# Four graph layers on one core: chunked normalising with ScalarE products at the end of the message layer, and a rearranged prologue of the polynomial layer

## What is computed

```
def _L2_gnn_ref(mu, x, edge_index, edge_w, W1, W2, W3, W4):
    ...
    agg = jax.ops.segment_sum(cat_feat, src, num_segments=n_nodes)
    agg = relu(agg @ W4.T)
    return relu(h_x + h_mu + agg)

def _L3_gnn_ref(x, W, bias, edge_index, num_nodes):
    ...
    deg = jax.ops.segment_sum(ones, row, num_segments=num_nodes)
    dinv = jnp.where(deg > 0, 1.0 / jnp.sqrt(jnp.where(deg > 0, deg, 1.0)), 0.0)
    norm = dinv[row] * dinv[col]

    def L_apply(h):
        msg = norm[:, None] * h[col]
        return h - jax.ops.segment_sum(msg, row, num_segments=num_nodes)
    ...
    for k in range(K + 1):
        out = out + h_k @ W[k] * inv_f
        if k < K:
            h_k = -T * L_apply(h_k)
            inv_f = inv_f / (k + 1)
    return out + bias
...
x = _layernorm(x + _L2_gnn_ref(x, node_vec1, edge_index, edge_weight, ...), axis=-1)
x = _layernorm(x + _L3_gnn_ref(x, L3_gnn_W, L3_gnn_bias, edge_index, 3125), axis=-1)
```

## Time and profile before

| what | value |
|---|---|
| median of three runs | 1601.18 us |
| profiled execution, own time | 1603.67 us |
| its span, first to last instruction | 1601.5 us |
| mean granted TensorE clock | 0.961 of full |
| TensorE busy | 1395.6 us (87%) |
| VectorE busy | 1232.4 us (77%) |
| ScalarE busy | 594.9 us (37%) |
| GpSimd busy | 44.4 us (3%) |

### The profile page before, as it was taken

The page is one execution under the profiler, slowest core; times in us unless marked ns, Lnnn a source line. Parts: engine busy times, 40 slices in busy tenths (PEclk is TensorE's granted clock), DMA queues, the critical chain, the costliest instruction groups (busy, mean ns, idle before and its releaser), DMA issues. The chain is left out here.

```text
span 1601.5 us, 44020 instructions
## 1 busy us (share of the span) xinstructions
PE 1395.6 (87%) x16795; PEld 1291.0 (81%) x16795; DVE 1232.4 (77%) x3606; ACT 594.9 (37%) x1073; POOL 44.4 (3%) x82
## 2 busy tenths in 40 slices
PE   0745468879987999999999979699999999999997
PEld 0434456669986888888888849599999999999997
DVE  4999988865446888888888867667777687677676
ACT  0249779971105777777777740100000000000000
POOL 2111100000000000000000000000000000000000
PEclk9989989989998999999999979689999999999999
DMA  1000035541005445454232260000000000000000
GB/s 20 9 1 0 0 91 157 158 129 33 2 15 152 127 133 153 114 152 114 83 106 75 63 152 2 6 2 2 2 2 2 2 2 2 2 2 2 2 6 19
DMA packets 37008, 83.91 MB, mean 52 GB/s; under 512 B 22941, under 2 KB 23957, under 8 KB 36863
## 3 DMA queue, kind: packets, MB, share of 16 engines
q1 hardware_dynamic: 33617, 81.46, 18.2%
q10 hardware_dynamic: 3024, 0.39, 0.2%
q0 software_dynamic: 224, 0.13, 0.1%
HBM read 60.76 MB, written 21.14 MB: 51 GB/s over the span
## 5 line engine op out<-in xcount | busy, mean ns | idle before, releaser
L1835 PE MATMUL L_psA<-L_parts,mat 125*128 125x192 bf16 x6250 | 517.1, 246 | 0.0
L1835 PEld LDWEIGHTS L_psA<-L_parts,mat 125*128 125x128 bf16 x6250 | 515.5, 98 | 1.0 <-DVE L_parts L1912 0.8
L1241 PEld LDWEIGHTS L_ps_pre<-L_drow,mat 128*128 128x128 bf16 x2250 | 128.8, 98 | 30.3 <-issue 1.1
L1774 ACT COPY L_wk<-L_Wk 128x64 f32 (+1 forms) x10 | 1.9, 242 | 391.6 <-PE L_psA L1835 391.6
L1899 DVE TENSOR_REDUCE L_sumr<-L_psA 125x64 f32<-125x192 f32 x225 | 80.5, 358 | 70.9 <-PE L_psA L1835 70.5
L1241 PE MATMUL L_ps_pre<-L_drow,mat 128*128 128x32 bf16 (+3 forms) x2250 | 133.1, 213 | 0.0
L690 PE MATMUL ps_count<-onehot 128*128 128x125 bf16 x1200 | 106.8, 218 | 17.0 <-DVE onehot L653 9.5
L1430 DVE TENSOR_TENSOR L_e<-L_e,mat 128x512 f32<-128x512 f32 x125 | 86.2, 689 | 39.2 <-ACT L_e L1328 39.2
L653 DVE TENSOR_TENSOR onehot<-iota_bf,codes 128x1024 bf16<-128x1024 bf16 x150 | 100.7, 688 | 17.9 <-PE ps_count L690 16.7
L891 PE MATMUL L_psA<-L_gparts,mat 125*128 125x192 bf16 x1250 | 109.3, 247 | 0.2 <-DVE L_sumr L995 0.2
L690 PEld LDWEIGHTS ps_count<-onehot 128*128 128x128 bf16 x1200 | 86.8, 98 | 25.1 <-DVE onehot L653 15.3
(11 more groups left out here) (314 smaller groups left out, 2279.4 us busy)
## 6 DMA issues: line engine op xcount, KB each, us to landing
L_drow<-rows_d SPq DMA_DIRECT2D x25, 728.0 KB
mat<-m_d SPq DMA_DIRECT2D x25, 684.2 KB
mat<-rows_d SPq DMA_DIRECT2D x25, 640.0 KB, 4.3
m_d<-panel SPq DMA_DIRECT2D x13, 684.2 KB
m_d<-xb SPq DMA_DIRECT2D x12, 684.2 KB
L_drow<-rows_d SPq DMA_DIRECT2D x25, 84.5 KB
mat<-m_d SPq DMA_DIRECT2D x25, 79.4 KB
m_d<-panel SPq DMA_DIRECT2D x13, 79.4 KB
```

Of the source, the lines that this page charges most:

```text
L1241: last = nc.tensor.matmul(ps_pre[bank][:, to:to + n], w, drow[k][:, of:of + n], start=False, stop=(r == 2 and cc == pieces[-1][0]))
L1835: last = nc.tensor.matmul(ps[:, 0:3 * D], t.mat[0:B, kb, b * B:b * B + P], parts[src][:, kb].rearrange("p r d -> p (r d)"), start=(kb == 0 ...
```

## The change

In the message layer:

- VectorE aggregates a block's statistics directly after taking them (`take_stats`: stats, wait, aggregate), one block earlier than before.
- The normalising is cut into five chunks of 6, 6, 6, 5 and 2 blocks. Two blocks after a chunk's last block, VectorE subtracts the mean for the chunk and takes the reciprocal (`centre`); the last chunks' come after the last block.
- ScalarE takes each chunk's root, multiplies each block by its reciprocal root into `t.xb`, waits for those products, and multiplies each by `t.scale` into `t.xa`, which is y of the polynomial layer. These are 2 x 25 instructions of 125 x 64 with a scale per partition.
- The degree mask, the degrees' roots and their reciprocals are worked out in the message layer, between its prologue and its first block.

In the polynomial layer:

- The degree work and the product over the whole tile are gone. TensorE's first two `turn`s wait for nothing; `zeroed` is waited for behind them.
- ScalarE scales the weights k = 8 and 9 early, and the others after the first staging; it takes over two of the six operations on each group, the copy into `y` and the cast to the middle part. VectorE has four left, and cuts the last part of a group after the first of the next.
- `scaled` has two buffers. Products of a group wait for the mask and the copy of group g-2 (`masked`, `y_kept`) instead of its parts, and so does the first staged product; the parts are waited for by the terms alone, as before per block.
- The first two staged weights are copied after the last group's `y` copy, ahead of the last middle cast.

The diff, cut to its core:

```diff
@@ -1583,7 +1584,20 @@
                         node_values(0)
                     if g + 1 < len(groups):
                         node_values(g + 1)
-                roots(nc, act, c, mv, std, var, root)
+                act.wait_ge(deg_set, 1)
+                nc.scalar.activation(t.root_deg[:], t.scale2[:], ACT.Sqrt).then_inc(droot, 1)
+                act.wait_ge(deg_step, 1)
+                for i, blocks in enumerate(chunks):
+                    act.wait_ge(var, i + 1)
+                    nc.scalar.activation(std[:, blocks], mv[:, blocks, 1], ACT.Sqrt, bias=c.eps[0:B, :]
+                                         ).then_inc(root, 1)
+                    act.wait_ge(centred, i + 1)
+                    for b in range(blocks.start, blocks.stop):
+                        last = nc.scalar.mul(t.xb[:, b, :], t.xa[:, b, :], rstd[:, b:b + 1])
+                    last.then_inc(x3_set, 1)
+                    act.wait_ge(x3_set, i + 1)
+                    for b in range(blocks.start, blocks.stop):
+                        nc.scalar.mul(t.xa[:, b, :], t.xb[:, b, :], t.scale[:, b:b + 1])
 
             @block.tensor
             def _(pe):
...
+                deg = t.wsum[:, :, WP - 1]
+                S(v.tensor_scalar(t.some[:], deg, 0.0, None, ALU.is_gt))
+                v.tensor_scalar(t.scale2[:], deg, 1.0, None, ALU.max).then_inc(deg_set, 1)
+                dve.wait_ge(droot, 1)
+                S(v.reciprocal(t.scale2[:], t.scale2[:]))
+                v.reciprocal(t.scale[:], t.root_deg[:]).then_inc(deg_step, 1)
+                ends = [blocks.stop - 1 for blocks in chunks]
+
+                def take_stats(b):
+
+                    S(v.bn_stats(bn[:, b, :], t.xa[:, b, :]))
+                    S.wait()
+                    last = v.bn_aggr(mv[:, b, :], bn[:, b, :])
+                    if b in ends:
+                        last.then_inc(var, 1)
+                    else:
+                        S(last)
+
+                def centre(i):
+
+                    blocks = chunks[i]
+                    dve.wait_ge(var, i + 1)
+                    S(v.tensor_tensor(t.xa[:, blocks], t.xa[:, blocks], mv[:, blocks, 0:1].broadcast_to(
+                        [B, blocks.stop - blocks.start, D]), ALU.subtract))
+                    dve.wait_ge(root, i + 1)
+                    S.wait()
+                    v.reciprocal(rstd[:, blocks], std[:, blocks]).then_inc(centred, 1)
+
                 dve.wait_ge(parts_ready, len(groups))
                 for b in range(NB):
                     r = sumr[b % 2][:]
@@ -1691,11 +1733,13 @@
                     S.wait()
                     v.scalar_tensor_tensor(t.xa[:, b, :], r, 0.0, t.xb[:, b, :], ALU.max, ALU.add).then_inc(kept, 1)
                     if b >= 1:
-                        S(v.bn_stats(bn[:, b - 1, :], t.xa[:, b - 1, :]))
-                    if b >= 2:
-                        S(v.bn_aggr(mv[:, b - 2, :], bn[:, b - 2, :]))
+                        dve.wait_ge(kept, b)
+                        take_stats(b - 1)
+                    if b >= 2 and b - 2 in ends:
+                        centre(ends.index(b - 2))
                 dve.wait_ge(kept, NB)
-                normalize(nc, dve, S, t.xa, bn, mv, std, rstd, t.xb, var, root, NB - 1, NB - 2)
+                take_stats(NB - 1)
+                centre(len(chunks) - 1)
...
+                    n = len(groups[g])
+                    act.wait_ge(turned, g + 1)
+                    nc.scalar.copy(x3T[0:D, 4 * g * B:(4 * g + n) * B].rearrange("p (b n) -> p b n", n=B),
+                                   psT[g % 2][0:D, 0:n * P].rearrange("p (b n) -> p b n", n=P)[:, :, 0:B]
+                                   ).then_inc(x3t, 1)
+
+                def keep_y(g):
+
+                    act.wait_ge(masked, g + 1)
+                    nc.scalar.copy(y[:, blocks_of(g), :], y_of(g)).then_inc(y_kept, 1)
+
+                def mid_part(g):
+
+                    act.wait_ge(cut, g + 1)
+                    nc.scalar.copy(parts[0][:, blocks_of(g), 1, :], scaled[g % 2][:, 0:len(groups[g]), :]
+                                   ).then_inc(mid_done, 1)
+
+                keep_columns(0)
+                act.wait_ge(w_in, 32)
+                scale_weights(KMAX).then_inc(wk_set, 1)
+                keep_columns(1)
+                for k in (KMAX - 2, KMAX - 1):
+                    last = scale_weights(k)
+                last.then_inc(wk_set, 1)
+                for g in range(len(groups)):
+                    if g + 2 < len(groups):
+                        keep_columns(g + 2)
+                    if g >= 1:
+                        mid_part(g - 1)
+                    keep_y(g)
                 act.wait_ge(wk_set, 2)
+                act.wait_ge(zeroed, 2)
                 stage(KMAX - 2)
+                mid_part(len(groups) - 1)
+                for k in range(1, KMAX - 2):
+                    last = scale_weights(k)
+                last.then_inc(wk_set, 1)
+                act.wait_ge(wk_set, 3)
                 with act.Fori(0, KMAX - 2, 2) as it:
...
-                pe.wait_ge(zeroed, 2)
-                pe.wait_ge(scaled_in, 1)
                 turn(0)
                 turn(1)
+                pe.wait_ge(zeroed, 2)
                 pe.wait_ge(wk_set, 1)
                 for g, blocks in enumerate(groups):
                     if g + 2 < len(groups):
                         turn(g + 2)
                     pe.wait_ge(x3t, g + 1)
                     if g >= 2:
-                        pe.wait_ge(parts_ready, 4 * (g - 1))
+                        pe.wait_ge(masked, g - 1)
+                        pe.wait_ge(y_kept, g - 1)
                     for i, b in enumerate(blocks):
                         last = nc.tensor.matmul(psY[g % 2][0:B, i * D:(i + 1) * D], x3T[:, b * B:(b + 1) * B],
...
+                pe.wait_ge(masked, len(groups))
+                pe.wait_ge(y_kept, len(groups))
 
                 def products(it):
...
                 dve.sem_inc(xw_used, 1)
-                deg = t.wsum[:, :, WP - 1]
-                S(v.tensor_scalar(some[:], deg, 0.0, None, ALU.is_gt))
-                v.tensor_scalar(safe[:], deg, 1.0, None, ALU.max).then_inc(deg_set, 1)
-                dve.wait_ge(droot, 1)
-                S(v.reciprocal(scale2[:], safe[:]))
-                S(v.reciprocal(scale[:], root_deg[:]))
-                S.wait()
-                v.tensor_tensor(y[:], t.xb[:], scale[:].unsqueeze(2).broadcast_to([B, NB, D]), ALU.mult
-                                ).then_inc(scaled_in, 1)
-                for g, blocks in enumerate(groups):
-                    n, b = len(blocks), blocks[0]
+
+                def cut_high(g):
+
+                    n, at, mine = len(groups[g]), scaled[g % 2][:, 0:len(groups[g]), :], blocks_of(g)
                     dve.wait_ge(y_ps, g + 1)
-                    if g:
-                        dve.wait_ge(parts_ready, 4 * g)
-                    y_in = psY[g % 2][0:B, 0:n * D].rearrange("p (b d) -> p b d", d=D)
-                    S(v.tensor_tensor(scaled[:, 0:n, :], y_in, some[:, b:b + n].unsqueeze(2).broadcast_to([B, n, D]),
-                                      ALU.mult))
-                    S(v.tensor_copy(y[:, b:b + n, :], y_in))
+                    if g >= 2:
+                        dve.wait_ge(parts_ready, 4 * (g - 1))
+                    v.tensor_tensor(at, y_of(g), some[:, mine].unsqueeze(2).broadcast_to([B, n, D]), ALU.mult
+                                    ).then_inc(masked, 1)
+                    dve.wait_ge(masked, g + 1)
+                    S(v.tensor_copy(parts[0][:, mine, 0, :], at))
                     S.wait()
-                    split(nc, S, lambda r: parts[0][:, b:b + n, r, :], scaled[:, 0:n, :], scaled[:, 0:n, :]
-                          ).then_inc(parts_ready, n)
+                    v.tensor_tensor(at, at, parts[0][:, mine, 0, :], ALU.subtract).then_inc(cut, 1)
+
+                def cut_mid(g):
+
+                    n, at, mine = len(groups[g]), scaled[g % 2][:, 0:len(groups[g]), :], blocks_of(g)
+                    dve.wait_ge(mid_done, g + 1)
+                    dve.wait_ge(cut, g + 1)
+                    v.tensor_tensor(parts[0][:, mine, 2, :], at, parts[0][:, mine, 1, :], ALU.subtract
+                                    ).then_inc(parts_ready, n)
+
+                for g in range(len(groups)):
+                    cut_high(g)
+                    if g >= 1:
+                        cut_mid(g - 1)
+                cut_mid(len(groups) - 1)
```

38 lines of the change are left out of this document (13 added, 25 removed).

## The result

The changed kernel takes 1596.65 us (median of 7 runs, 1593.93 to 1602.4), beside 1608.71 us (7 runs, 1600.2 to 1609.15) for the kernel before on the same chip: ratio 0.9958, 95% interval 0.9938 to 0.9978. The ratio compares executions side by side; it is not the quotient of the two medians (0.9925), which move by several us from set to set. A second set of 11 runs gave 1597.46 us and 0.9961 (0.9942 to 0.9979). So it is faster by 0.4%, and neither interval holds 1. By the ratio that is some 6.5 us; forecast were 7.3.

The account below looks back on a forecast made before the run. TensorE was taken to bound the message loop and last terms, so only the 34.5 us seam between layers could shrink: +0.5 - 5.0 - 2.9 + 0.1 = -7.3 us, giving 1593.9 us, range 1590.5 to 1597.0.

Parts of the forecast that it names:

- Part 1, the tail: Message layer's end, after the last reduction: ScalarE's small products replace VectorE's whole-tile operations; 0.5 us later.
- Part 2, behind the barrier: Start of the polynomial layer: transposes need only y, then the scaled top weight gates TensorE's restart; 5.0 us gained.
- Part 3, the groups: Polynomial prologue's seven groups, bound by TensorE: first staged product 16.2 us after restart instead of 19.1; 2.9 us gained.
- Part 4, elsewhere: Degree work moved into a VectorE wait, and chunk steps and waits in the message loop; 0.1 us charged, bounds 0 and 1.
- The chances: Odds for the whole kernel's measured time: faster 0.40, same 0.57, slower 0.03.
- late loads: Rival: behind the barrier, the weight loads' landing holds TensorE; half way, 1023.3, costs 2.4 us, giving 1596.3; 6%.
- slower products: Rival: ScalarE's products take 0.395 or more, or its queue holds the groups; 0.7 us in the tail, 1596.0; 6%.
- a VectorE-bound loop: Rival: new waits in each of 25 message blocks make VectorE the bound, from 0.33 us more per block; up to 1609.4; 3%.
- The clock: Rival: the tighter polynomial prologue raises TensorE's clock until VectorE bounds the groups; 4.7 us more gained, 1589.2; 7%.

Follow-up runs that it names:

- kernel 3: The change, but VectorE instead of ScalarE does both products of the last two chunks, one instruction per chunk and product; 1593.99 us in one run.
- Kernel 4: The change with the message layer's normalising cut into 13 chunks of two blocks, the last of one; 1592.46 us in one run.
- kernel 5: The change, but the bias has its own semaphore, so the scaling of the top weight waits for the weights alone; 1596.90 us in one run.
- kernels 6: The change, but weights loaded in the message layer into a tile already cleared, and no GpSimd clearing behind the barrier; 1595.19 us in one run.
- kernel 10: The change with weights loaded in the message layer and no clearing behind the barrier, run a second time; 1596.92 us, ratio 0.9931 to before.
- kernel 1: The change's polynomial prologue with the message layer of before; degree work and y at the prologue's head; 1599.65 us, ratio 0.9962 to before.
- 7: The change with chunks of two blocks, weights loaded in the message layer and no clearing behind the barrier; 1593.36 us, ratio 0.9928 to before.
- kernel 9: Message layer of before, the change's prologue with y at its head, weights loaded early, no clearing behind the barrier; 1599.11 us, ratio 0.9962 to before.
- 8: The changed kernel run again without alteration; 619.78 us from the 4th message-loop reduction to the program's last reciprocal, in one trace.

## Why the prediction was right or wrong

The median of 1596.65 lies within the range of 1590.5 to 1597.0, near its end, and 2.75 above the forecast. In the trace, 6.5 us are gained where I said 7.3. Against the 1601.18 from which I had started, the median is only 4.5 less, but that start was the median of three runs of a scattering time: the medians of before beside the experiments were 1608.71, 1603.92, 1605.03 and 1604.45. So that the time itself lies in the range is in part luck. The ratios, taken side by side, agree with the trace (0.4% is 6.4 us; the whole distance is 6.6 us shorter).

- **Part 1, the tail**: forecast +0.5, measured +0.54. A 125x64 product takes 0.333 us in the median (forecast 0.345), five take 1.30 (1.3). The price stood on the earlier trace rows alone and held. The Trainium skill (ScalarE: Activation LUTs, Rules for kernel authors) says to multiply on VectorE; kernel 3 agrees in direction and ends the tail 1.64 us sooner, less than the 2 to 3 us that I had read from it: VectorE is done with the five blocks at 1012.22 (1011.73 + 0.49), but the last chunk's statistics, subtraction, reciprocal and products stand behind them on the same engine and end at 1013.82.
- **Part 2, behind the barrier**: forecast -5.0, measured -4.71. The DMA rates from 1026 to 1028, in slots of 0.05 us, show the last packets until 1026.85:

```profile
GB/s 36 36 21 20 20 26 20 26 15 10 20 26 20 26 21 15 15 0 0 0 0 0 0 0 0 0 0 0 0 0 0 0 0 0 0 0 0 0 0 0
```

  ScalarE started 0.35 later; I had taken 0.15, and 0.3 from there to the restart, which took 0.35. The packets took as long as those of the earlier trace rows: they end 3.44 us behind the issue of the weights, 3.43 there (1017.32 to 1020.75).
- **Part 3, the groups**: forecast -2.9, measured -2.84. Period 2.41 (2.42), with VectorE idle before each of the groups 1 to 4.
- **Part 4, elsewhere**: forecast +0.1, measured +0.52. **This step of the sum failed.** I wrote "the write ends 1.52 after its reduction starts (1010.78 to 1012.30) against a period of 2.13 (53.30/25), which leaves 0.6 less the hand-over: barely enough". The 2.13 holds the slow start of the loop; from the 4th to the 25th reduction a block takes 43.32/21 = 2.06. And the weight load of a block runs ahead of its products, so it feels the lateness first: the one at 1009.94 would have started at 1009.71, and without the chunk's push of 0.46 us the row would have been written at 1009.43, so the room was 0.28 and not 0.6. Three waits of 0.23 us are the 0.7 in the trace, of which 0.52 reach the last reduction. Kernel 4 bears it out: steps of 128 columns instead of 384 leave no wait.
- **The chances**: this is where the prediction went wrong outright. I put 57% on no difference that can be told, because I set that bound at 0.5% (8.0 us) and my own forecast at 0.46%. The spread of single runs (1600 to 1609) is that large, but the comparison is not that coarse: both sets exclude 1, with half-widths of 0.2%. A forecast of 7.3 us against an uncertainty of some 3 us is a forecast of faster. The failed step is "just under the 0.5% (8.0 us) that a measurement of this kernel can tell from no change".
- **The rivals**: late loads (the landing 0.20 us later than I took it, not 2.4), slower products and a VectorE-bound loop did not come. The last has a grain of truth: VectorE reached TensorE three times, through the chunks and not through the pair of waits in each block. The clock did not rise within the groups of the changed kernel in either of its traces. The Trainium skill's rule (TensorE: Matmul & The Clock Gate, Part 1: activity releases the throttle) is not borne out there: the granted clock is 0.50 from 1027.50 to 1043.80, in which TensorE is busy for 13.72 us of 16.30. In kernels 5, 6 and 10 it did rise, and the groups became bound by VectorE and ScalarE, as the rival said: the restart to the staged product took 14.24 us in kernel 5 instead of 16.26.

What the prediction did not ask is what each half is worth. It priced the message part as 0.5 + 0.1 of cost and part 2 as one gain of 5.0, without saying that up to the first product 3.3 of 4.7 us are had by the prologue's own reordering, since the loads end about where y ends.

## What to carry to other kernels

When an input is made ready sooner, look for the next gate before giving it a price: here the transposes could start 3.6 us earlier and 1.4 reached the products, because a load and a clearing behind the same barrier ended there; moving the load gave the earlier y its worth. And look at what a gate is for: some 2.6 us of kernel 1's gain came from a root that had stood behind a clearing it did not need. Slack within a loop is to be taken from its steady part, against the longest step put between two blocks, and from the weight loads' point of view. Where single executions scatter more than the change, compare stretches between fixed places in the traces, and take the measurement's uncertainty from the interval of a side-by-side ratio, not from the scatter.

## What the runs showed of the hardware

**The clock in the prologue depends on more than the code.** The transposes and group products of kernels 6, 7 and 10 are the same instructions, as dense in each: TensorE stood idle 7.17, 5.37 and 7.16 us before them and the clock was at its 1.2 GHz level when they began. In 6 and 10 it rose some 3.6 us later, during the first group's products (eight in 1.47 and 1.46 us instead of 1.78), in 7 not within 17.5 us. In kernel 9 (9.98 us idle, 17.8 us of work) it did not rise either. Why is open; the two traces of one kernel agreed each time (change and 8: low; 6 and 10: high), and no run varied the idle time by itself. Among all traces with the new prologue those that rose (5, 6, 10) had 7.2 us of idle time before it and then no stop, or one of 1.66 us; those with 5.4 to 5.6 us of idle time (3, 4, 7), with 10 us (1, 9), or with a stop of 2.24 us (change and 8) stayed low. That is an observation, not a cause.

**A clock that rises in the prologue can be given back in part.** In kernel 10 it fell again at about 1034.0, after TensorE had begun to wait between the groups, and over the next 4.50 us TensorE was busy for 1.73; the staged products then ran at 0.50 for the whole 5.50 us from 1038.50, against 4.00 us at 0.53 in the change. They take 8.30 us there, 7.98 in kernel 7 and 7.37 in the change. With kernel 7's groups and its own tail kernel 10 would stage at 6.83 + 18.15 = 24.98; it stages at 22.17. So of 2.8 us gained 0.3 are lost again beside kernel 7. In kernel 5, where the clock also fell before the staged products, it rose again sooner and they take 6.91 us. The medians (1596.92 and 1593.36) and ratios (0.9931 and 0.9928) of kernels 10 and 7 do not bear on it: kernel 7 has the shorter tail and loop instead of the clock, and over the whole distance the two are alike, 615.40 and 615.54 us.
